# Second retention of a two-layer retention and expert kernel: q, k and gate from halves, one output product, root and sum interleaved

## The reference

```python
def _msr_forward(x, Wq, Wk, Wv, W1, W2, gn_w, gn_b):
    xh = x.reshape(B, S, HEADS, HEAD)              # 8 heads of 16
    q = jnp.einsum('bshd,hde->bshe', xh, Wq)       # k and v likewise
    scores = jnp.einsum('bnhd,bmhd->bhnm', q, k) * D[None]   # D: causal decay
    ret = jnp.einsum('bhnm,bmhd->bnhd', scores, v)
    ret = (ret - mu) * jax.lax.rsqrt(var + EPS)    # per head
    ret = ret.reshape(B, S, HIDDEN) * gn_w + gn_b
    gated = x @ W1
    out = gated * jax.nn.sigmoid(gated) + ret
    return out @ W2
```

## Time and profile before

| | us |
|---|---|
| median of 3 runs (lowest to highest) | 1362.58 (1361.58 to 1368.63) |
| the profiled execution | 1365.58, its span 1363.4 |
| second retention | about 577 to 939 of the span |
| granted TensorE clock, mean | 0.91 of 2.4 GHz |

### The profile page before, as it was taken

The page is one execution under the profiler, slowest core; times in us unless marked ns, Lnnn a source line. Parts: engine busy times, 40 slices in busy tenths (PEclk is TensorE's granted clock), DMA queues, the critical chain, the costliest instruction groups (busy, mean ns, idle before and its releaser), DMA issues. The chain is left out here.

```text
span 1363.4 us, 33977 instructions
## 1 busy us (share of the span) xinstructions
PE 1144.9 (84%) x10118; PEld 1035.0 (76%) x10119; DVE 914.1 (67%) x2697; ACT 708.8 (52%) x1621; POOL 762.1 (56%) x1070
## 2 busy tenths in 40 slices
PE   7999999993299999468999999852999999999900
PEld 6899999983299999446777767642999999999900
DVE  4789888873466666247888877634766666666447
ACT  2344444432266666245666665532666666666525
POOL 0267777775368887611466666574344444444467
PEclk9999999985599999779999998955999999999955
DMA  8111112010433333142321120013111111111166
GB/s 259 40 58 57 47 39 78 28 32 28 110 88 101 98 99 98 53 141 78 94 84 49 56 89 29 29 40 87 48 55 54 54 54 54 54 54 55 32 188 193
DMA packets 81527, 101.70 MB, mean 75 GB/s; under 512 B 15154, under 2 KB 59698, under 8 KB 81010
## 3 DMA queue, kind: packets, MB, share of 16 engines
q1 hardware_dynamic: 55730, 60.96, 15.7%
q0 software_dynamic: 17280, 35.69, 8.0%
q10 hardware_dynamic: 8448, 4.20, 1.1%
HBM read 60.93 MB, written 44.11 MB: 77 GB/s over the span
## 5 line engine op out<-in xcount | busy, mean ns | idle before, releaser
L1068 POOL DMA_INDIRECT expert_out<-e_ysb,e_idx x284 | 285.3, 1005 | 91.3 <-issue 83.3
L1228 PE MATMUL banks<-e_x_hi,e_w_hi 128*128 128x256 f32 x852 | 254.8, 299 | 0.6 <-DVE e_h L1199 0.4
L1228 PE MATMUL banks<-e_x_lo,e_w_hi 128*128 128x256 f32 x852 | 242.5, 285 | 0.0
L1228 PE MATMUL banks<-e_x_hi,e_w_lo 128*128 128x256 f32 x852 | 242.5, 285 | 0.0
L1240 PE MATMUL banks<-w_dn,e_h 128*128 x1704 | 213.6, 275 | 0.0
L1240 PEld LDWEIGHTS banks<-w_dn,e_h 128*128 128x128 f32 x1704 | 203.4, 193 | 0.0
L1199 DVE TENSOR_TENSOR e_h<-banks,e_sgl 128x512 f32<-128x512 f32 x213 | 146.3, 687 | 78.5 <-PE banks L1228 76.3
L1094 ACT ACTIVATE e_sgl<-banks 128x512 f32<-128x512 f32 x213 | 127.5, 599 | 120.4 <-PE banks L1228 110.0
L1228 PEld LDWEIGHTS banks<-e_x_hi,e_w_hi 128*128 128x128 f32 x852 | 164.3, 193 | 5.8 <-issue 1.6
L1228 PEld LDWEIGHTS banks<-e_x_lo,e_w_hi 128*128 128x128 f32 x852 | 164.7, 193 | 0.0
L1228 PEld LDWEIGHTS banks<-e_x_hi,e_w_lo 128*128 128x128 f32 x852 | 164.3, 193 | 0.0
(11 more groups left out here) (275 smaller groups left out, 2581.6 us busy)
## 6 DMA issues: line engine op xcount, KB each, us to landing
e_xg<-scattered SPq DMA_DIRECT2D x142, 130.0 KB, 2.1
b_cy<-expert_out SPq DMA_DIRECT2D x32, 256.0 KB, 2.9
f_y<-expert_out SPq DMA_DIRECT2D x32, 256.0 KB, 3.0
expert_out<-e_ysb,e_idx POOLq DMA_INDIRECT x284, 2.3
a_xb<-in_x SPq DMA_DIRECT2D x16, 256.0 KB, 2.9
out<-f_x ACTq DMA_DIRECT2D x16, 256.0 KB, 2.5
scattered<-in_spare SPq DMA_DIRECT2D x2, 1040.0 KB, 6.2
scattered<-in_spare SPq DMA_DIRECT2D x16, 130.0 KB, 2.9
```

The source lines that it names most:

```text
L1068: nc.gpsimd.indirect_dma_start(out=expert_out, out_offset=bass.IndirectOffsetOnAxis(ap=idx[d.slot][:, i:i + 1], axis=0), in_=ysb[d.slot][: ...
L1228: mm = nc.tensor.matmul(banks[bank_of(j, c)][:, i * ROWS:(i + 1) * ROWS], w_[c.slot][:, g, f:f + P], x_[c.slot][:], start=(k == 0), stop=( ...
```

## The change

- `InverseRoot.compute` is taken apart into links; a new function `root_beside_sum` issues root (of c1) and sum (of y) alternately, and stands ahead of the second masks. In steps without one of the two, root and sum are as before, the sum also ahead of the masks.
- q, k and gate are made of halves: ScalarE writes `x_hi` (fp32r, a rounded copy) ahead of `xT`, GpSimd subtracts `x_lo` = xT - x_hi ahead of its second scatter pair, the weights are split once in the set-up, and `by_halves` issues three products where two f32 passes stood.
- The gate moves behind the first scores on TensorE.
- The output product is one product of `oT` with `w_2`: VectorE makes `og` = T1 * gn_w * oc and, behind the router's operations, `oT` = og + gn_b + sgT. The products with `sgT`, `w2g` and the two halves of `gn_b @ W2` go, with what set them up. ScalarE's `sgT` waits for `oT_there` instead of `y_mm`, its `oc` for `t_made`.

`made` and `ready` are the two halves of the old `Chain.link`: the first lets an operation signal, the second waits for that signal. `root.begin`, `estimate`, `square`, `halved` and `better` are the lines L196 to L203 of before, each ending in `made`; `first_part(c)` and `second_part(c)` are L1294 and L1308 for chunk c. The core of the diff (the set-up of the halves of the weights and the names are left out):

```diff
                     def paced(y, a, b, c1, c2, d, e):
                         if e:
                             router.scatter_pair(pool, e, 0)
+                        if a:
+                            pool.wait_ge(xT_ev, a.n + 1)
+                            nc.gpsimd.tensor_tensor(x_lo[a.odd][:], xT[a.odd][:], x_hi[a.odd][:].bitcast(F32), ALU.subtract
+                                                    ).then_inc(x_lo_there, 1)
+                        if e:
                             if d:
                                 router.scatter_pair(pool, e, 1, router.lg_mm, d.n + 1)
...
                             act.wait_ge(xT_mm, a.n + 1)
+                            nc.scalar.copy(x_hi[a.odd][:], T0[:, :])
                             nc.scalar.copy(xT[a.odd][:], T0[:, :]).then_inc(xT_ev, 1)
                             nc.scalar.copy(xres[:, bass.ds(a.n * CH, CH), :], xb[a.odd][:]).then_inc(x2_kept, 1)
                         if d:
...
                             act.wait_ge(g_mm, b.n + 1)
 
-                            wait_count(act, y_mm, b.n - 1)
+                            wait_count(act, oT_there, b.n - 1)
                             nc.scalar.activation(sgT[b.odd][:], T1[:, :], ACT.Silu).then_inc(sg_there, 1)
                         if c1:
 
...
                             wait_count(act, var_mm, b.n)
                             nc.scalar.activation(osq[:], O[:, :], ACT.Square).then_inc(sq_there, 1)
-                            wait_count(act, oT_there, b.n)
+                            wait_count(act, t_made, b.n)
                             nc.scalar.copy(oc[:], O[:, :]).then_inc(oc_there, 1)
                         if d:
                             router.tanh_of(act, d)
...
 
+                    def root_beside_sum(c1, y):
+                        comb.wait_loaded(dve, y)
+                        root.begin(dve, var, c1)
+                        comb.first_part(0, y)
+                        root.chain.ready()
+                        root.estimate()
+                        comb.first_part(1, y)
+                        root.chain.ready()
+                        root.square()
+                        comb.first_part(2, y)
+                        root.chain.ready()
+                        root.halved()
+                        comb.chain.start(dve, y)
+                        comb.chain.made(comb.first_part(3, y))
+                        root.chain.ready()
+                        root.better()
+                        comb.chain.ready()
+                        comb.chain.end()
+                        comb.second_part(0, y)
+                        root.chain.ready()
+                        root.square()
+                        comb.second_part(1, y)
+                        root.chain.ready()
+                        root.halved()
+                        comb.second_part(2, y)
+                        root.chain.ready()
+                        root.better()
+                        comb.second_part(3, y).then_inc(comb.used, 1)
+                        for i in range(root.ROUNDS - 2):
+                            root.chain.ready()
+                            root.square()
+                            root.chain.ready()
+                            root.halved()
+                            root.chain.ready()
+                            root.better()
+                        root.chain.ready()
+                        root.chain.end()
+                        dve.wait_ge(comb.used, y.n + 1)
+
                     def residual(c2):
                         dve.wait_ge(y_mm, c2.n + 1)
...
                             dve.wait_ge(var_there, c1.n + 1)
-                            root.compute(dve, var, c1)
+                        if c1 and y:
+                            wait_count(dve, x2_there, y.n - 1)
+                            root_beside_sum(c1, y)
+                        else:
+                            if c1:
+                                root.compute(dve, var, c1)
+                            if y:
+                                wait_count(dve, x2_there, y.n - 1)
+                                comb.sum(dve, y)
                         if b:
                             masked_scores(b, 1)
-                        if y:
-
-                            wait_count(dve, x2_there, y.n - 1)
-                            comb.sum(dve, y)
                         if c2 and b:
                             residual(c2)
                         if a:
...
                             dve.wait_ge(oc_there, c1.n + 1)
+                            nc.vector.scalar_tensor_tensor(og[:], T1[:, :], g_w[:, 0:1], oc[:], ALU.mult, ALU.mult
+                                                           ).then_inc(t_made, 1)
+                        if d:
+                            router.choose(dve, LG, d)
+                        if d:
+                            router.rows_of(dve, RK, d)
+                        if c1:
+                            dve.wait_ge(t_made, c1.n + 1)
+                            dve.wait_ge(sg_there, c1.n + 1)
 
                             wait_count(dve, y_mm, c1.n)
-                            nc.vector.tensor_tensor(oT[:], T1[:, :], oc[:], ALU.mult).then_inc(oT_there, 1)
-                        if d:
-                            router.choose(dve, LG, d)
-                        if d:
-                            router.rows_of(dve, RK, d)
+                            nc.vector.scalar_tensor_tensor(oT[:], og[:], g_b[:, 0:1], sgT[c1.odd][:], ALU.add, ALU.add
+                                                           ).then_inc(oT_there, 1)
 
                     dve.wait_ge(s_early, n_w)
...
+                    pe.wait_ge(lo_there, 3)
+
+                    def by_halves(to, hi, lo, t):
+                        nc.tensor.matmul(to[:], hi[:], x_hi[t.odd][:], start=True, stop=False)
+                        nc.tensor.matmul(to[:], hi[:], x_lo[t.odd][:], start=False, stop=False)
+                        return nc.tensor.matmul(to[:], lo[:], x_hi[t.odd][:], start=False, stop=True)
...
-                        pe.wait_ge(sg_there, c2.n + 1)
-                        nc.tensor.matmul(T0[:].rearrange("p (c d) -> p c d", c=CH), ones_r[:],
-                                         gb_hi[:].unsqueeze(1).to_broadcast([1, CH, D]), start=True, stop=False,
-                                         skip_group_check=True)
-                        nc.tensor.matmul(T0[:].rearrange("p (c d) -> p c d", c=CH), ones_r[:],
-                                         gb_lo[:].unsqueeze(1).to_broadcast([1, CH, D]), start=False, stop=False,
-                                         skip_group_check=True)
                         for i in range(CH):
-                            nc.tensor.matmul(T0[:, i * D:(i + 1) * D], sgT[c2.odd][:, i * P:(i + 1) * P], w_2[:],
-                                             start=False, stop=False, skip_group_check=True)
-                            mm = nc.tensor.matmul(T0[:, i * D:(i + 1) * D], oT[:, i * P:(i + 1) * P], w_2g[:],
-                                                  start=False, stop=True, skip_group_check=True)
+                            mm = nc.tensor.matmul(T0[:, i * D:(i + 1) * D], oT[:, i * P:(i + 1) * P], w_2[:],
+                                                  start=True, stop=True)
                         mm.then_inc(y_mm, 1)
 
                     def body(ts):
                         _, _, a, b, c1, c2, d = ts
                         if b:
-
-                            wait_count(pe, oT_there, b.n - 1)
-                            wait_count(pe, sg_there, b.n)
-                            nc.tensor.matmul(T1[:], w_1[:], xT[b.odd][:], start=True, stop=True).then_inc(g_mm, 1)
                             pe.wait_ge(qx_there, b.n + 1)
                             pe.wait_ge(kT_there, b.n + 1)
                             pe.wait_ge(v_ev, b.n + 1)
                             pe.wait_ge(kt_ev, b.n + 1)
                             scores(b, 0)
+
+                            wait_count(pe, t_made, b.n - 1)
...
-                            nc.tensor.matmul(B[0][:], w_q[:], xT[a.odd][:], start=True, stop=True)
-                            nc.tensor.matmul(B[1][:], w_k[:], xT[a.odd][:], start=True, stop=True).then_inc(qk_mm, 1)
+                            pe.wait_ge(x_lo_there, a.n + 1)
+                            by_halves(B[0], hi_q, lo_q, a)
+                            by_halves(B[1], hi_k, lo_k, a).then_inc(qk_mm, 1)
                         if b:
                             pe.wait_ge(S_there, b.n + 1)
```

More of the change, by code:

```diff
@@ L191, in __init__, with begin, estimate, square @@
                 self.chain = Chain(sem(name + "_chain"))
[L193 to L194 removed]
+            def begin(self, dve, v, t):
                 self.chain.start(dve, t)
                 nc.vector.tensor_scalar(self.half[:], v[:], -0.5, None, ALU.mult)
[L197 to L203 removed]
```

(35 more changed lines are left out.)

63 lines of the change are left out of this document (27 added, 36 removed).

## The result

The kernel after takes 1396.53 us (median of 4 runs, 1395.59 to 1400.16), the kernel before 1364.01 on the same chip (median of 4 runs): ratio 1.0245, 95% interval 1.021 to 1.0279, slower. The profiled execution took 1396.22 for a span of 1394.3. The forecast was 1390, slower, range 1366 to 1410.

A forecast was written before the change was run, and what follows sets the result against it. A four-engine loop through VectorE, ScalarE, GpSimd and the scatter transfer was taken to set the 18.56 us step. Steady steps 14.6, steps without scatters 4.5, filling 3 and clock 5 gave 27: 1393 profiled, 1390 median, range 1366 to 1410.

The forecast's parts named there:

- X: Second retention, time from b_var until the second masks start: 2.87 us before, forecast 4.1, or 5.2 with blocking by x_lo.
- In the queue x_lo costs nothing: GpSimd: x_lo moves the second scatter pair by 0.4 us, but that pair is done before the masks are.
- 14.82 + 5.2 = 20.0: Steady step closed by the loop through masks, GpSimd's third scatter pair and powers, transfer and router: 20.0 us for 18.56.
- C: Experiments' theory, not the prediction's: added work (og, oT, x_lo) and the clock are the cost, not the block.
- the 12.5 of the TensorE loop: Steps without scatters: from q and k's start, when the masks end, to the next b_var, 12.5 us; about 11.2 without router.
- Only partly reaches the longer loop: TensorE's clock ahead of q: a fall costs up to 1.5 us per step; bounds 0 and 20, 5 taken in total.
- the rival: TensorE's clock falls in every step, 13 x 1.5 = 20 us: 1405 us, chance 0.13.
- the rivals: Fallen clock at 816 costs nothing any more, -4 us: parts cancel (1362, chance 0.09) and faster (1353, chance 0.08).
- Steps 4 to 6: Three steps without scatters, 620.96 to 672.85, closed by TensorE's loop: 17.3 to 18.8 us each, 4.5 in all.
- Filling: Start of the second retention: first q and k wait for x_hi, x_lo and two hand-overs; 3 us.
- The output product: TensorE: dropped products save 1.6 us per step, on neither loop, so counted as zero.
- The signs named ahead: Steady part: 20.0 us step, third pair waits, powers don't, one long link, TensorE idle 3 us, clock under 1.00, no sgT wait.

The follow-up runs named there:

- e1: Kernel after with x_lo made behind GpSimd's second scatter pair instead of ahead of it; 1387.47 us, ratio to before 1.0199.
- e6: Kernel after with q, k and gate as whole f32 products again, without x_hi and x_lo; ratio to before 1.0185.
- e2: Kernel after with the old VectorE order: root, then second-half masks, then sum; 1380.32 us, ratio to before 1.0147.
- e3: Kernel after with across(b) and within(b, 1) ahead of TensorE's wait for the masks; 1388.04 us, ratio to before 1.0206.
- e4: Kernel after with 12 filling 128x56 products in TensorE's idle time ahead of q; 1386.66 us, ratio to before 1.0183.
- e10: Kernel before with q, k and gate by halves and x_lo on GpSimd ahead of the second scatter pair; ratio to before 1.0107.
- e5: Kernel after with the second half's masks ahead of the alternating block of root and sum; ratio to before 1.0085.
- e8: Kernel before with the one output product, og and oT made on VectorE; ratio to before 0.9952.
- e7: Kernel before with the root's links alternating with the sum ahead of the second half's masks; ratio to before 1.0075.
- e9: e8 with the gate's product moved behind the scores of the first half; ratio to before 1.0027.
- e12: e8 with yb's transposes ahead of TensorE's mask wait and GpSimd's fourth scatter pair ahead of both powers; 1350.62 us, ratio to before 0.99.
- e11: e8 with the alternating block of root and sum, placed behind the second half's masks; ratio to before 1.0075.
- the second and third group: Runs e5 to e8 and e9 to e11, in which the kernel before took 1481.84 and 1468.81 us.

## Why the prediction was right

*The block and x_lo: right.* X was put at 4.1, and 5.2 with blocking. Measured are 4.17 without a stopped link (e1, e6) and 5.26 with one. The Trainium skill ("SBUF — State Buffer", "Who interferes with whom") says that a VectorE instruction with two SBUF inputs and a GpSimd instruction that reads SBUF contend. The traces agree: an operation with two SBUF inputs is stopped by `x_lo` in the steady steps of after, e2, e3, e4 and e10, a link at 1.18 to 1.31 for 0.18 or a sum operation at 1.35 to 1.45 for 0.34, and the masks of e5, with one, are not. The row that the prediction took the price from, `f_n_neg` at 1.18, has one SBUF input and is not this case; that its size fitted is partly luck.

*What I missed about it:* x_lo stops a link of the root in the old order as well (e2, e10). The price belongs to the halves and not to the meeting of halves and block. The halves alone cost (1.0107 - 1) x 1468.8 = 15.7 us, the added falls of e10 included. "In the queue x_lo costs nothing" held: the third pair still waits 1.71 for the masks.

*The step: right in size, and a near miss in its loop.* The forecast closed the step through GpSimd: 14.82 + 5.2 = 20.0. At full clock that is so, 19.7 (e3, e4), with `b_r_x` waiting for its transfer. In the kernel as it is another loop closes, over TensorE: masks 2.41 from their start to q, then 762.20 is reached without idle but 0.56, and `b_var` 12.67 behind q: 5.26 + 2.41 + 12.67 = 20.34. `b_r_x` is done at 761.46, 0.74 before TensorE turns to it. VectorE is no earlier: in five of the nine steady steps, this one too, `b_var` starts without a wait, straight behind `b_S` (763.09), and VectorE's queue holds 0.8 us more work by `og` and `oT` (0.75 each for one of 0.69). No run takes that work out of the kernel after, so a share of C in its 20.7 is not ruled out; e8, where the same work costs nothing (18.3), and e6, where `b_var` always waits 0.67 and the step is 20.9, speak against a large one. The prediction had the 12.5 of the TensorE loop in hand and used it, cut down, only for the steps without scatters.

*The clock: the mis-sized term.* "Only partly reaches the longer loop", 5 us of 0 to 20. The clock fell in every steady step, as the rival had it, but at 1.0 a step (e4; 1.1 to 1.5 in e1) and not 1.5. Ten steady steps went from 189.3 (`b_var` 667.08 to 856.36) to 206.8 (681.44 to 888.22): 10 x (19.7 - 18.5) = 12 by the late masks where I had 14.6, 10 x 1.0 = 10 by the falls, less the 4 that a fall had cost the kernel before in one step (22.6). That is 18 for a measured 17.5. Of the 12, e1 puts nearly all on the stopped link: without it, at full clock, the step is 18.6. That the total came near is partly luck: the falls cost twice the 5 that I took, but the late masks cost less than forecast, and the kernel before paid 4 for a fall of its own that only the rivals counted. The Trainium skill ("TensorE: Matmul & The Clock Gate", section "HAM oscillation — how this bites in real kernels") says that idle stretches between bursts bring the throttle back, burst after burst. The trace of after agrees, with a fall in each step behind 3.5 us of idle time, and e7, whose TensorE waits at most 1.0 for the masks, has none in its steady steps. It does not explain all: the longer falls of e3, e4 and e10 begin 0.5 to 1.5 us behind `b_var`, while TensorE is busy.

*Steps 4 to 6:* 9.2 (51.3 to 60.5), 4.5 forecast. The stopped link is there (1.28 at 622.67 and 643.54), and the granted clock is 0.84 in the first two. *Filling:* 5.1 against 3. *The output product* "as zero": alone it gives 7.1 us back (e8).

*How the parts add.* The block alone costs 0.0075 x 1481.8 = 11.1 us. On top of the one product and the gate's place (e9 to e6) it costs 27.4 - 4.0 = 23.4: without the long product TensorE has nothing to do while the masks are late (2.4 us ahead of q in e6), and the clock falls in each step, where e7 has no fall. So the part that the prediction counted as free, the shorter product, costs nothing alone and probably makes the block about twice as dear, through the clock. Not shown is how much of that is the gate's new place: no run has the block with the one product and the gate where it was. Each of these differences is uncertain by some 6 us, and the experiments ran on three chips.

The signs named ahead came out: third pair waiting for `b_sT`, no wait ahead of the powers, one link over 1 us, TensorE 3.5 idle ahead of q, `sgT` without a wait. The step was to be 20.0; it is 20.3 in the step shown and 20.7 in the median.

## What to carry to other kernels

Before work is taken off an engine that "has slack", look at which wait it covers: here TensorE's removed products had kept it busy while the masks were late, and with them gone its clock fell. A whole-tile GpSimd operation on SBUF is to be priced at its full length for whatever VectorE issues beside it with two SBUF inputs, however small; moved out of the way (e1) it left a step of 18.6 wherever the clock held. Where an engine waits for a transfer, look for compute in front of the transfer in the issuing queue that could stand behind it: that move, together with its earlier signal, took the step from 18.3 to 17.6 (e12).

## What was not expected of the hardware

- A stopped operation waits for all of the other: 128x32 operations of 0.18 us last up to 1.31, until `x_lo` ends. `x_lo` itself takes 1.26 to 1.28 where it meets only small links (e10), and 1.41 where it starts while a sum operation runs (after).
- The granted clock falls for about 3 us in some steps (all but one of the nine in after, all in e1, e2 and e6) and for 7 to 10 in others (before, e3, e10, e11, and single steps of after, e4 and e5). Some falls have no long idle time of TensorE just ahead of them: those of e3, e4 and e10 from 0.5 to 1.5 us behind `b_var` on, and those of e6 at the gate, behind 1.2 to 1.3 us. What sets these off is open.
- In the second and third group the kernel before takes 1469 to 1482. In the trace of e9 the granted clock is 0.86 from 100 to 150 us, in the first retention, where it is 1.00 in e12 on the same chip. That the clock is the whole cause is not shown: by it alone a seventh less work would be done, and TensorE's products are a quarter fewer (345 for 459).

```profile
100.00:150.00 50.00, 46.88 (x345) 42.58 (x343) 35.14 (x110) 19.08 (x35) 30.00 (x35) 0.86 0.17 53
```

```profile
100.00:150.00 50.00, 49.90 (x459) 46.40 (x459) 43.41 (x153) 20.26 (x35) 36.67 (x50) 1.00 0.17 52
```
